# The layer norm's apply on GpSimd, and its statistics in other PSUM banks

## What is computed

```python
def _layernorm(x, axis=-1, eps=1e-5):
    m = jnp.mean(x, axis=axis, keepdims=True)
    v = jnp.var(x, axis=axis, keepdims=True)
    return (x - m) / jnp.sqrt(v + eps)

# attention, xn = _layernorm(x)
    scores = jnp.einsum('bsnd,btnd->bnst', q, k) * D[None]
    ret = jnp.einsum('bnst,btnd->bsnd', scores, v)
    norm = (ret - mean) / jnp.sqrt(var + 1e-05)          # group norm per head
    norm = norm.reshape(b, s, h) * gn_scale + gn_bias
    gate = jnp.matmul(x, w1)
    out = gate * jax.nn.sigmoid(gate) + norm
    return jnp.matmul(out, w2)

# layer
    x = x + attn(_layernorm(x), ...)
    x = x + ffn(_layernorm(x), ...)                      # router, 8 experts, shared expert
```

## Time and profile before

| | |
|---|---|
| median of the runs | 1912.4 us (1910.78 to 1914.02) |
| profiled execution | 1915.89 us, span of the slowest core 1914.3 us |
| spans of the eight cores | 1896.9 to 1914.3 us |
| TensorE busy | 1534.4 us, 80% |
| VectorE busy | 812.4 us, 42% |
| ScalarE busy | 378.6 us, 20% |
| GpSimd (POOL) busy | 24.9 us, 1%, in 34 instructions |
| granted TensorE clock | 0.839 of full speed |

### The profile page before, as it was taken

How to read it: one execution, slowest core, us unless ns; L and a number is a source line. 1 busy time by engine, 2 the same in 40 slices (tenths; PEclk the granted TensorE clock), 3 DMA queues, 4 the chain that set the end, 5 groups by cost and what they waited for, 6 DMA issues and landing times.

```text
span 1914.3 us, 20879 instructions; the slowest of 8 cores (1896.9 to 1914.3 us)
## 1 busy us (share of the span) xinstructions
PE 1534.4 (80%) x7156; PEld 616.4 (32%) x7156; DVE 812.4 (42%) x1534; ACT 378.6 (20%) x683; POOL 24.9 (1%) x34
## 2 busy tenths in 40 slices
PE   0665776677577566999899999999999999999960
PEld 0221222122122123444343344444444444444420
DVE  0376577567656653222233233333333333332333
ACT  2423232242232111100111111111111111111100
POOL 1000000000000000000000000000000000000000
PEclk9755765675576567999999999999999999999985
DMA  9000020020000035002302222022221302223015
GB/s 144 6 1 1 0 45 1 0 45 1 1 0 23 1 55 100 1 1 29 60 1 45 44 45 45 1 45 45 44 45 19 69 2 45 45 45 67 1 66 175
DMA packets 41352, 67.26 MB, mean 35 GB/s; under 512 B 3858, under 2 KB 16530, under 8 KB 41250
## 3 DMA queue, kind: packets, MB, share of 16 engines
q0 software_dynamic: 26432, 48.65, 15.7%
q1 hardware_dynamic: 14818, 17.29, 2.8%
HBM read 101.96 MB, written 12.58 MB: 60 GB/s over the span
## 4 chain that ended last, share of the span: by engine, by line
PE 62%; DMA 15%; DVE 11%; issue 4%; DVEq 4%; ACT 2%; POOL 0%; ACTq 0%; SPq 0%; POOLq 0%
PE P L1257 18%; PE P L1289 18%; DMA we_sb<-we 11%; PE P L666 3%; PE P L1122 3%; PE P L1175 3%; PE P L1133 3%; PE P L713 3%; PE P L451 3%; PE P L918 3%; DMA xj<-x 2%; DVEq L97 2%; DVE s_sb L697 2%; DMA x1rl<-x1s 2%; DVEq L887 1%
## 5 line engine op out<-in xcount | busy, mean ns | idle before, releaser
L1257 PE MATMUL P<-x2st,we_sb 128*128 128x512 bf16 x2048 | 452.3, 382 | 11.5 <-DMA we_sb<-we 11.5
L1289 PE MATMUL P<-htil,we_sb 128*128 128x512 bf16 x1984 | 436.3, 381 | 11.6 <-DMA we_sb<-we 11.6
L1268 ACT ACTIVATE hs_scr<-P 128x512 bf16<-128x512 f32 x256 | 152.9, 597 | 773.8 <-PE P L1257 773.8
L1257 PEld LDWEIGHTS P<-x2st,we_sb 128*128 128x128 bf16 x2048 | 198.9, 98 | 257.1 <-issue 25.8
L1301 DVE TENSOR_TENSOR acc<-acc,P 128x512 f32<-128x512 f32 x248 | 170.5, 688 | 258.3 <-PE P L1289 258.3
L1289 PEld LDWEIGHTS P<-htil,we_sb 128*128 128x128 bf16 x1984 | 194.4, 98 | 249.6 <-issue 18.9
L1275 DVE TENSOR_TENSOR htil<-hs_scr,bcomb 128x512 bf16<-128x512 bf16 x256 | 108.8, 425 | 355.0 <-ACT hs_scr L1268 355.0
L713 PE MATMUL P<-s_sb,vst 128*64 128x512 bf16 (+3 forms) x128 | 57.7, 451 | 49.4 <-DVE s_sb L697 49.3
L451 PE MATMUL P<-xlnj,w1a_sb 128*128 128x512 bf16 x256 | 67.4, 423 | 28.3 <-DVE xlnj L391 26.4
L690 DVE SCALAR_TENSOR_TENSOR s_sb<-P,gmn_sb,masks_sb 128x512 bf16<-128x512 f32 (+3 forms) x128 | 70.1, 547 | 36.8 <-PE P L672 36.0
L666 PE MATMUL P<-qt,kst 64*128 64x512 bf16 x128 | 73.4, 586 | 13.8 <-DVE ktok L598 6.7
(11 more groups left out here) (167 smaller groups left out, 1263.5 us busy)
## 6 DMA issues: line engine op xcount, KB each, us to landing
we_sb<-we POOLq DMA_DIRECT2D x16, 2048.0 KB, 14.8
out<-acc SPq DMA_DIRECT2D x4, 2048.0 KB, 8.1
xj<-x POOLq DMA_DIRECT2D x4, 1024.0 KB, 24.4
x1s<-xj SPq DMA_DIRECT2D x4, 1024.0 KB, 5.9
wgu_sb<-wgu POOLq DMA_DIRECT2D x1, 4096.0 KB, 31.9
x1rl<-x1s SPq DMA_DIRECT2D x4, 1024.0 KB, 10.3
w1a_sb<-w1a POOLq DMA_DIRECT2D x1, 2048.0 KB, 21.5
w2a_sb<-w2a POOLq DMA_DIRECT2D x1, 2048.0 KB, 34.3
```

The source lines that it names most:

```text
L1257: last = e.matmul(bank[:, :], we1_sb[:, 1024 * k + 128 * f:1024 * k + 128 * f + 128], x2st[:, ST * k + 512 * j:ST * k + 512 * j + 512], st ...
L1268: e.activation(hs_scr[:, hsl:hsl + 512], bank[:, :], AF.Silu),
L1289: last = e.matmul(bank[:, :], we2_sb[:, 1024 * f + 128 * m:1024 * f + 128 * m + 128], htil[:, pslot + 512 * f:pslot + 512 * f + 512], star ...
```

## The change

Two things. The apply of every layer norm (L386, L391) goes from VectorE to GpSimd, and in it both subtractions now come ahead of both multiplications; the first subtraction also waits for the reciprocal, and each multiplication waits for its own half's subtraction. And the statistics of the next pass's LN1 go to the banks P4 and P5 instead of P0 and P1, with waits to match: the statistics wait for the last eviction of the retention's result, the group norm's first broadcast no longer waits for the finished statistics, and the first projection matmuls into P4 and P5 wait for them.

```diff
@@ -379,23 +379,21 @@
                 in3 = xj[:, xoff:xoff + 4096].rearrange("p (c t) -> p c t", t=512)
-                marks = []
-                for h in (0, 1):
-                    def a1(e, h=h):
-                        with nc.allow_low_precision(reason="bf16 LN apply"):
-                            return e.tensor_tensor(mid[:, 4 * h:4 * h + 4, :],
-                                                   in3[:, 4 * h:4 * h + 4, :],
-                                                   mu_b, ALU.subtract)
-                    def a2(e, h=h):
-                        with nc.allow_low_precision(reason="bf16 LN apply"):
-                            return e.tensor_tensor(out3[:, 4 * h:4 * h + 4, :],
-                                                   mid[:, 4 * h:4 * h + 4, :],
-                                                   rs_b, ALU.mult)
-                    m_a1 = p.do("vector", a1,
-                                waits=[m_evmu, guard] if h == 0 else [],
-                                mark=True)
-                    m_a2 = p.do("vector", a2, waits=[m_a1, m_rec], mark=True)
-                    marks.append(m_a2)
+                def a1(e, h):
+                    with nc.allow_low_precision(reason="bf16 LN apply"):
+                        return e.tensor_tensor(mid[:, 4 * h:4 * h + 4, :],
+                                               in3[:, 4 * h:4 * h + 4, :],
+                                               mu_b, ALU.subtract)
+                def a2(e, h):
+                    with nc.allow_low_precision(reason="bf16 LN apply"):
+                        return e.tensor_tensor(out3[:, 4 * h:4 * h + 4, :],
+                                               mid[:, 4 * h:4 * h + 4, :],
+                                               rs_b, ALU.mult)
+                m_a1h = [p.do("gpsimd", lambda e, h=h: a1(e, h),
+                              waits=[m_evmu, m_rec, guard] if h == 0 else [],
+                              mark=True) for h in (0, 1)]
+                marks = [p.do("gpsimd", lambda e, h=h: a2(e, h),
+                              waits=[m_a1h[h]], mark=True) for h in (0, 1)]
                 prev_lnapply = marks[1]
                 return [marks[0]] * 4 + [marks[1]] * 4
@@ -843,11 +841,10 @@
                 if j + 1 < nj:
-                    ln1_ctx = ln_partA(m_x_next, P[0], P[1],
+                    ln1_ctx = ln_partA(m_x_next, P[4], P[5],
                                        xoff=4096 * ((j + 1) % 2),
                                        bufs=(ln1_f, ln1scr, ln1_b),
-                                       first_waits=list(prev_sev[0] or ()) +
-                                                   list(m_qkev[7]))
+                                       first_waits=[m_retj_ev[7]])
                     hoist_fin = ln1_ctx[1]
@@ -874,9 +871,6 @@
                     m_b = p.do("tensor", gnb,
                                waits=[m_gfin, m_selb, prev_gnb[c % 3]] +
                                      ([m_ktevA_last] if c == 2 else []) +
-                                     ([hoist_fin,
-                                       ln1_ctx[3] if j + 1 < nj else None]
-                                      if c == 0 else []) +
                                      list(prev_sev[0] or ()) +
                                      list(prev_sev[1] or ()), mark=True)
@@ -897,10 +891,12 @@
                     if c >= 3:
-                        omk01(0, c - 3, extra=([prev_op[0]] if c == 3
-                                               else []))
-                        omk01(1, c - 3, extra=([prev_op[1]] if c == 3
-                                               else []))
+                        omk01(0, c - 3, extra=([prev_op[0], hoist_fin]
+                                               if c == 3 else []))
+                        omk01(1, c - 3,
+                              extra=([prev_op[1]] +
+                                     ([ln1_ctx[3]] if j + 1 < nj else [])
+                                     if c == 3 else []))
```

## The result

The changed kernel takes 1.0394 times the time of the one before, 95% interval 1.0359 to 1.0429; a second set of executions gave 1.0427 (1.0387 to 1.0467). On the 1912.4 us of before that is +75 us (69 to 82), and +82 (74 to 89) the second time. The forecast was 1999 us, +87; the executions of the first set took 1986 to 2006 us. The traced core is core 3 here and core 1 before; on core 1 the spans are 1985.2 and 1914.3 us.

A forecast was written before the change was run, and what follows sets the result against it. TensorE was taken to bound the last 60%, untouched; in the first 740 us waits on single chains count. Terms 49.8 + 24.8 + 12.3 + 6.7 - 9.9 + 3 = +86.7 us gave a median of 1999 us, range 1960 to 2045.

The forecast's parts named there:

- one operation on POOL: Price G of one two-input apply operation on GpSimd: 4.3 us, two reads in turn with the write under them.
- LN1, four times: From reciprocal to second half's gate matmuls, 17.45 us instead of 4.99 at each LN1: 49.8 us in all.
- LN2 under the gates, three times: Passes 0 to 2: the next pass's value matmul waits for LN2 on POOL, 0.8 given back: 24.8 us.
- last LN2: Nothing covers this apply; reciprocal's end to apply's end takes 17.35 us instead of 5.08: 12.3 us.
- load of wgu: Queued behind the last LN2 apply on POOL, it lands late and the barrier after the router waits: 6.7 us.
- banks: Group norm no longer waits for LN1's statistics; its first apply starts 3.3 us earlier in three passes: -9.9 us.
- clock: The twelve gate matmuls behind the second wait run partly at TensorE's lower clock after longer idling: +3 us.
- 32G - 50.9: The summed change in us as a function of G, the price of one apply operation on POOL.
- the two handovers: Added to 4G between LN1's reciprocal and the second half's gate matmuls: 0.25 us.
- The rivals with 2.1 and 6.2 us as the price: POOL's streams at once, G 2.1, +15.9 us, chance 0.08; three in a row, G 6.2, +147.5 us, chance 0.11.
- the rival of a clock that stays low: All 48 gate matmuls at 0.44 instead of 0.22 us in four passes: +129 us, 2041 us; chance 0.05.

The follow-up runs named there:

- experiments 3: The changed kernel with LN2's apply back on VectorE in its old order, LN1's staying on GpSimd: 1.0177 times the kernel before.
- experiment 1: The kernel before with only LN1's statistics moved to banks P4 and P5 and matching waits, apply on VectorE: ratio 0.9948, second set 0.9934.
- experiment 5: The changed kernel with value matmuls waiting only for the reads of LN2's broadcast banks, not its applied result: 1.0297 times the kernel before.
- experiment 4: The changed kernel with the load of wgu ahead of the last LN2 apply on GpSimd's queue: 1.0348 times the kernel before, second set 1.0335.
- experiment 7: The changed kernel with each apply's first half on VectorE and second on GpSimd at the same time: two executions, 1946.6 and 1948.3 us.

## Why the prediction was right

Each term against the traces, in us:

| step | forecast | measured |
|---|---|---|
| one operation on POOL | 4.3 | 4.01 from start to start, 4.05 long |
| LN1, four times | +49.8 | +45.4 (4 x 11.36); experiments 3 and 1: 45 |
| LN2 under the gates, three times | +24.8 | +23.0; experiment 5: 19 to 25 |
| last LN2 | +12.3 | +11.1 |
| load of wgu | +6.7 | +7.4; experiment 4: 9 and 18 |
| banks | -9.9 | -11.2; experiment 1: -10 and -13 |
| clock | +3 | about +1 in the passes' LN2 term, and +0.6 in the first pass |
| sum | +86.7 | +75.7 from the traces; +75 and +82 by time |

The terms leave little over. The first gate-up matmul comes at 818.89 instead of 738.67 us, 80.2 later, in the traced core; on core 1 of the same execution it comes at 813.75, 75.1 later than on core 1 before. Of the traced core's 4.5 us that stand in no term, 1.2 are there before the first LN1 and 0.6 in the first pass's gate; the rest is spread over the stretches between, and how much of it is chance between cores stays open.

*The price of POOL's operation.* The forecast of 4.3 us was near the 4.01 measured, but the way to it is not shown: no run changes the number of inputs, so that the two reads follow each other and the write hides under them stays a guess. It was picked as the middle between 2.1 and 6.2, from an iota that reads nothing; that it came within 0.3 us is in part luck. It was 0.3 us too dear, and with the two handovers (0.25 assumed, 16.35 - 4 x 4.01 = 0.31 measured) the formula 32G - 50.9 gives 77 us at G = 4.01. That one step makes nearly all the difference between 87 and 76. The rivals with 2.1 and 6.2 us as the price are out. What the Trainium skill states for fp32 in "GPSIMD Engine Reference" (section "Performance versus the Vector engine"), 4497 ns, lies on the same side; these 16-bit operands take 4.05 us. VectorE's side is 1.22 us here, so GpSimd takes 3.3 times as long.

*LN2 under the gates.* The stretch from the second half's gate matmuls to the cross matmul, in the second pass before:

```profile
232.66 4.85 PE L451 MATMUL P<-xlnj,w1a_sb 128*128 128x512 bf16 x12 [0.59 <-DVE xlnj L391]
...
251.27 0.40 PE L622 MATMUL P<-qt,Ms_b 64*64 64x512 bf16 x1
```

and in the changed kernel:

```profile
252.40 5.28 PE L449 MATMUL P<-xlnj,w1a_sb 128*128 128x512 bf16 x12 [2.14 <-POOL xlnj L389]
...
279.69 0.63 PE L620 MATMUL P<-qt,Ms_b 64*64 64x512 bf16 x1
```

That is 18.6 and 27.3 us, +8.7; in the fourth pass 18.2 and 24.9, +6.7; the third pass lies between with +7.6. The cross matmul follows its value matmul sooner than before by 0.72 us in the second and third pass (2.15 to 1.43) and by 1.38 in the fourth (1.82 to 0.44), where 0.8 was assumed: that part was about right, and what made the term too dear is G.

*The last LN2 and the load.* From the reciprocal's end (769.27) to the apply's end (785.47) are 16.2 us, 5.08 before. From there to the gate-up matmul are 818.89 - 785.47 = 33.4 us, 26.0 before: 7.4. The load landed after 33.3 us, not 31.9, which is the difference to the 6.7 forecast but for some tenths.

*The banks.* The retention's last eviction of the third pass, before and in the changed kernel:

```profile
497.49 0.69 DVE L747 CAST retj<-P 64x512 bf16<-64x512 f32 x1 [0.57 <-PE P L718]
...
543.96 0.69 DVE L745 CAST retj<-P 64x512 bf16<-64x512 f32 x1 [0.57 <-PE P L716]
```

From the start of that eviction to that of LN1's reciprocal the three passes became shorter by 5.2, 1.8 and 4.3 us (the last from 555.22 - 497.49 = 57.7 to 597.39 - 543.96 = 53.4). The step named VectorE's variance (L338) as what comes next, and it does. The scatter between the passes goes with TensorE's granted clock, and was not forecast: over these stretches it was 0.66, 0.70 and 0.66 before and 0.71, 0.67 and 0.70 now. Where the clock is nearly alike, the gain is 3.3 us (57.8 at 0.66 and 54.5 at 0.67) and 2.8 us (56.3 and 53.4 at 0.70), close to the 3.3 forecast.

*The clock.* The twelve gate matmuls behind the second wait take 5.28 and 4.11 us in the second and fourth pass, 4.85 and 3.25 before: +0.4 and +0.9. The 48 that follow take 10.65 us in three passes, as before, and 11.05 instead of 10.72 in the first, so the rival of a clock that stays low is out.

## What to carry to other kernels

An engine that is idle is not free: before moving an operation, ask whether a chain waits for its end, and count its latency on the new engine once per place where nothing covers it. Then look at what else stands on that engine's queue, as here the load of 4 MB behind the last apply, and at waits written wider than needed, which a fast engine hides and a slow one does not. What gained here was a change that moved no work, only the banks that two chains shared.

## What the runs showed of the hardware that was not expected

Halving an elementwise job between VectorE and GpSimd gave no parallel time at all when both sides read two SBUF inputs: 2 x 1.22 + 2 x 4.05 = 10.5 us if one after another, 10.1 measured (experiment 7). In the trace a blocked operation looks slow, 4.89 us for one of 1.22, and not late: the time in which it is blocked is counted as busy. GpSimd's two-input operation ran at its full rate, 4.05 us, beside VectorE's evictions from PSUM (experiment 5) and beside the load of 4 MB (experiment 4), and its first one in the program was no slower than the others (4.04 us in the changed kernel).
